# An attention product in fp32 with one set of weights, the mask on VectorE, the shift on GpSimd, a router product with stacked weights, and another opening and order

## The reference, cut to what matters

```python
x = x + tanh(g_xattn) * xattn(LN(x), ctx)
x = x + tanh(g_ffn)  * ffn(LN(x))
# xattn: q = Wq x + bq; k, v = Wk ctx + bk, Wv ctx + bv; 8 heads of 32 channels,
#        each position attends to a window of 16 positions; softmax; Wo out + bo
# ffn, each of the 16*256 rows of 2048 positions is a token:
logits  = flat @ router_weight.T + router_bias      # 64 experts
scores  = softmax(logits); topk_w, topk_idx = top_k(scores, 8)
out     = flat * topk_w.sum() + w_dense @ expert_bias
```

## Time and profile before

| | us |
|---|---|
| median of 3 runs | 1567.97 |
| profiled execution, its time | 1567.15 |
| its span, first to last instruction | 1565.0 |
| PE busy | 1469.5 (94%) |
| PE weight loads busy | 1210.0 (77%) |
| DVE / ACT / POOL busy | 1269.8 / 1148.2 / 1148.8 |
| mean granted TensorE clock | 0.981 |

### The profile page before, as it was taken

One profiled execution on the slowest core, in us unless ns is written; L12 is line 12 of the kernel. 1 busy time (PEld: TensorE's weight loads), 2 busy tenths in 40 slices (PEclk: granted clock), 3 DMA queues, 4 the chain that ended last, 5 costly groups with the idle time before them and its releaser, 6 DMA issues.

```text
span 1565.0 us, 66658 instructions
## 1 busy us (share of the span) xinstructions
PE 1469.5 (94%) x28162; PEld 1210.0 (77%) x28162; DVE 1269.8 (81%) x2970; ACT 1148.2 (73%) x2009; POOL 1148.8 (73%) x1110
## 2 busy tenths in 40 slices
PE   2599999999999999999999999999999999999985
PEld 1477887888888888888888887888888788778764
DVE  4377887889888888988888898888889888888864
ACT  3488777778777877877777787777778787767752
POOL 2487877777787878778787777878777787867762
PEclk8799999999999999999999999999999999999997
DMA  6354455554555455455545545554554555434232
GB/s 202 97 143 125 133 138 133 156 150 102 176 139 136 135 157 142 109 177 139 129 139 157 141 111 179 137 131 137 154 146 110 169 144 132 124 85 132 64 73 93
DMA packets 365577, 210.39 MB, mean 134 GB/s; under 512 B 294497, under 2 KB 295521, under 8 KB 361057
## 3 DMA queue, kind: packets, MB, share of 16 engines
q1 hardware_dynamic: 365280, 206.14, 48.6%
HBM read 136.88 MB, written 33.55 MB: 109 GB/s over the span
## 4 chain that ended last, share of the span: by engine, by line
PE 60%; DVE 26%; issue 7%; POOL 2%; ACT 2%; DMA 1%; SPq 1%; POOLq 0%; DVEq 0%; ACTq 0%
PE ps_j L1099 22%; PE ps_a L1123 9%; PE ps_s L1158 9%; PE ps_s L1099 6%; PE ps_r L1200 6%; DVE prob_t L882 3%; DVE wq_lo L805 2%; PE ps_s L1153 2%; DVE p_sum L872 2%; PE ps_t L1140 2%; PE ps_a L1177 2%; DVE lg L1028 2%; DVE neg_max L861 1%; DVE st_x L889 1%; DVE v_turn L853 1%
## 5 line engine op out<-in xcount | busy, mean ns | idle before, releaser
L474 POOL TENSOR_TENSOR score<-score,p_inv 128x384 f32<-128x384 f32 x256 | 221.8, 867 | 117.2 <-DVE p_inv L876 116.1
L481 POOL TENSOR_TENSOR prob<-score,prob 128x384 f16<-128x384 f32 x256 | 266.1, 1040 | 30.8 <-ACT prob L633 30.0
L1158 PEld LDWEIGHTS ps_s<-kv_win,q_col 32*32 32x32 f32 x16384 | 192.9, 105 | 55.2 <-issue 55.2
L1123 PEld LDWEIGHTS ps_a<-prob_t,v_diag 128*128 128x128 f16 x6528 | 198.9, 97 | 42.3 <-DVE prob_t L882 26.2
L1123 PE MATMUL ps_a<-prob_t,v_diag 128*128 128x64 f16 (+1 forms) x6528 | 212.4, 190 | 19.4 <-DVE prob_t L882 16.0
L1158 PE MATMUL ps_s<-kv_win,q_col 32*32 32x48 f32 x16384 | 228.2, 203 | 1.9 <-issue 1.9
L455 POOL TENSOR_TENSOR c_lo<-c_in,c_hi 128x1024 fp32r<-128x1024 f32 x64 | 152.5, 2382 | 98.6 <-ACT c_hi L607 98.6
L882 DVE STREAM_TRANSPOSE prob_t<-prob 128x512 f32<-128x512 f32 x256 | 176.7, 699 | 54.9 <-POOL prob L481 54.9
L1099 PE MATMUL ps_j<-c_hi,wkv_hi 128*128 128x512 f32 x512 | 170.9, 415 | 39.9 <-POOL c_lo L455 29.9
L450 POOL TENSOR_TENSOR att_lo<-att,att_hi 128x512 fp32r<-128x512 f32 x128 | 162.7, 1275 | 60.2 <-ACT att_hi L593 59.4
L571 ACT ACTIVATE kv_win<-ps_j,v_bias 128x512 f16<-128x512 f32 x128 | 106.5, 844 | 109.7 <-PE ps_j L1099 109.7
(11 more groups left out here) (149 smaller groups left out, 3320.6 us busy)
## 6 DMA issues: line engine op xcount, KB each, us to landing
v_diag<-v_turn SPq DMA_DIRECT2D x512, 68.0 KB, 2.8
c_in<-ctx_dram SPq DMA_DIRECT2D x64, 512.0 KB, 4.8
x_in<-x_dram SPq DMA_DIRECT2D x64, 512.0 KB, 5.6
x_res<-x_dram SPq DMA_DIRECT2D x64, 512.0 KB, 4.4
out_dram<-x SPq DMA_DIRECT2D x32, 1024.0 KB, 7.0
c_sq<-ctx_dram SPq DMA_DIRECT2D x60, 512.0 KB, 5.5
x<-ctx_dram SPq DMA_DIRECT2D x4, 512.0 KB, 6.5
x<-experts_dram SPq DMA_DIRECT2D x2, 512.0 KB, 10.9
```

The lines of the kernel that those rows point to most:

```text
L474: pool.tensor_tensor(score[:, u], score[:, u], p_inv[:, u, :].unsqueeze(2).to_broadcast([P, HALF, KEYS]), ALU.mult).then_inc(pm_rdy, 1)
L481: pool.tensor_tensor(part(prob[:, u % 2], 1)[:, :, 0:KEYS], score[:, u], part(prob[:, u % 2], 0)[:, :, 0:KEYS], ALU.subtract).then_inc(pl_ ...
L1123: ins = pe.matmul(ps_a[g][:, q0:q1], part(v_diag[:, g, j], kv), part(prob_t[:, g, lo:hi], kp), start=(j == 0 and n == 0), stop=(j == NB), ...
L1158: ins = pe.matmul(s[head(h), n * KEYS:(n + 1) * KEYS], q_col[head(h), g, at:at + SUB], kv_win[c % 2][head(h), 0, g, at:at + KEYS], start=F ...
```

## The change

- `attend` uses the whole fp32 words of `v_diag` and `prob_t`: one fp32 matmul for each of the 17 blocks, of 48 columns (all but the first leave out 16 columns that the window never reaches). The f16 halves go, and with them `high`, `low`, `values_low`, the squares of ctx with their loads, `scales` and the rescaled weights of v.
- The mask is no longer a matmul: the bank is opened by a bf16 matmul of zeros of 2 columns, and DVE adds the mask while it copies the scores to SBUF (`masked`); the maximum is taken there, and `shift` goes to POOL.
- The router works on float32r halves: ACT and DVE write `turn_hi` and `turn_lo`, the stationary operand is `wr_both` (high and low weights of the 64 experts side by side), the moving one has 256 columns. The two halves of the result are added by a product with `fold` once a sequence (`logit_sums` on ACT, `fold_logits` on PE).
- The sum of the router's weights is one matmul of a sum made by DVE instead of 16; splitting the experts goes from POOL to ACT and DVE.
- The opening loads v's weights, c_in, k's weights and x first, and waits for no scale. The order on every engine is another, `queries(1)` stands at the end of the step before instead of at the start of its own, and each unit has semaphores of its own.

```diff
 def attend(g, off):
     for j in range(BLKS):
-        lo = max(0, (2 * j - 1) * SUB)
-        q0 = max(0, (j - 1) * SUB)
-        for n, (kv, kp) in enumerate(((0, 0), (1, 0), (0, 1))):
-            ins = pe.matmul(ps_a[g][:, q0:q1], part(v_diag[:, g, j], kv),
-                            part(prob_t[:, g, lo:hi], kp),
-                            start=(j == 0 and n == 0), stop=(j == NB), skip_group_check=True)
+        skip = SUB // 2 if j else 0
+        lo = max(0, (2 * j - 1) * SUB) + skip
+        q0 = max(0, (j - 1) * SUB) + skip
+        ins = pe.matmul(ps_a[g][:, q0:q1], v_diag[:, g, j], prob_t[:, g, lo:hi],
+                        start=(j == 0), stop=(j == NB), skip_group_check=True)
 def scores(u, off):
-    pe.matmul(s[:, 0:HALF * KEYS], ident_b[:], mask[:].rearrange("p n k -> p (n k)"),
+    pe.matmul(s[:, HALF * KEYS:HALF * KEYS + 2], blank[:], blank[:, 0:2],
               start=True, stop=False, skip_group_check=True)
 def router(off):
     for k in range(TB):
-        for g in range(G):
-            ins = pe.matmul(ps_r[:, g * E:(g + 1) * E], x1_t[:, g, k], wr[:, ch * TB + k], ...)
+        for n, v in enumerate((turn_hi, turn_lo)):
+            ins = pe.matmul(ps_r[:, ACC], wr_both[:, ch * TB + k], v[:, k].rearrange("p g c -> p (g c)"), ...)
+def fold_logits():
+    need(pe, acc_rdy, b)
+    for g in range(G):
+        ins = pe.matmul(ps_r[:, LOGITS + g * E:LOGITS + (g + 1) * E], acc[:, g * P:(g + 1) * P], fold[:], ...)
...
 # DVE
-def shift(u):
-    dve.tensor_tensor(score[:, u], scores_of(u), neg_max[:, u, :].unsqueeze(2).to_broadcast([P, HALF, KEYS]), ALU.add)
+def masked(u, off):
+    need(dve, s_mm[u], nth(b, c, off))
+    need(dve, pt_rdy[u], nth(b, c, off - 1))
+    dve.tensor_tensor(score[:, u, :, 0:KEYS], ps_s[u % 2][:, 0:HALF * KEYS].rearrange("p (n k) -> p n k", k=KEYS),
+                      mask[:].unsqueeze(1).to_broadcast([P, HALF, KEYS]), ALU.add).then_inc(mk_rdy[u], 1)
+def turned_low(g, off):
+    dve.tensor_tensor(turn_lo[:, :, g], ps_t[:].rearrange("p (k t) -> p k t", k=TB), turn_hi[:, :, g], ALU.subtract)
...
 # POOL
-def low(u):
-    pool.tensor_tensor(part(prob[:, u % 2], 1)[:, :, 0:KEYS], score[:, u], part(prob[:, u % 2], 0)[:, :, 0:KEYS], ALU.subtract)
+def shift(u, off):
+    pool.tensor_tensor(rows, rows, neg_max[:, u, :].unsqueeze(2).to_broadcast([P, HALF, KEYS]), ALU.add)
...
```

More of the change, by code:

```diff
@@ L33 @@
 BF16 = mybir.dt.bfloat16
-F16 = mybir.dt.float16
 I32 = mybir.dt.int32
@@ L310, in head @@
             return slice(SUB * h, SUB * (h + 1))
[L312 to L316, removed]
         OWN = slice(LEFT, LEFT + CHUNK)
+        wr_staged = x1[1][:, 1, 0:(T // P) * E].rearrange("p (n e) -> p n e", e=E)
+        ex_staged = x1[1][:, 0, :]
+        wo_staged = att[:, :, 0:C]
         block = stack.enter_context(nc.Block())
@@ L513, in step @@
+                if live(b, c, 0):
+                    shift(1, 0)
+                    normalise(0, 0)
+                if live(b, c, -1):
+                    residual(0, -1)
+                    residual(1, -1)
+                if live(b, c, 0):
+                    shift(2, 0)
+                if live(b, c, 1):
+                    x_low(1)
+                if live(b, c, 0):
+                    shift(3, 0)
+                    normalise(1, 0)
                 if live(b, c, 1) or live(b, c, 2):
@@ new lines, in step @@
+                if live(b, c, 0) and live(b, c, 4):
+                    next_stats(0)
+                if live(b, c, -2):
+                    turned_low(1, -2)
+                if live(b, c, 0) and live(b, c, 4):
+                    next_stats(1)
+                if live(b, c, 0):
+                    masked(1, 0)
+                if live(b, c, 0) and c == 3 and seq(b + 1):
+                    ln1(b + 1)
+                if live(b, c, 0):
+                    largest(1, 0)
+                    values_turn(0, 0)
+                    total(0, 0)
+                    invert(0, 0)
@@ L933, in step @@
+                if c == 1 and seq(b - 1):
+                    router_logits(b, 0)
+                if live(b, c, 0):
+                    values_turn(1, 0)
+                if c == 1 and seq(b - 1):
+                    router_logits(b, 1)
                 if finishing(b, c):
                     finish(0)
-                if now:
-                    largest(2)
-                    shift(2)
+                if c == 1 and seq(b - 1):
+                    router_logits(b, 2)
+                if live(b, c, 0):
+                    masked(2, 0)
@@ L1263, in step @@
                     mixture(1)
-                if before:
-                    output(0)
-                    output(1)
-                if now:
-                    scores(3)
+                if c == 1 and seq(b - 1):
+                    fold_logits()
+                if live(b, c, 0):
+                    scores(2, 0)
+                if live(b, c, -1):
+                    output(0, -1)
+                    output(1, -1)
+                if live(b, c, 0):
+                    scores(3, 0)
+                if live(b, c, 2):
+                    values(0, 2)
+                    values(1, 2)
+                if live(b, c, -1):
+                    rows(0, -1)
+                if live(b, c, 2):
+                    keys(0, 2)
                 if finishing(b, c):
@@ L1271, in step @@
                 if live(b, c, 2):
-                    values(0)
-                    values(1)
+                    keys(1, 2)
+                if live(b, c, 1):
+                    queries(0, 1)
                 if finishing(b, c):
@@ L1276, in step @@
                 if live(b, c, 1):
-                    queries(0, 1)
-                if before:
-                    rows(0, -1)
-                if live(b, c, 2):
-                    keys(0)
-                    keys(1)
-                if b == -1 and c == 3:
-                    pe.wait_ge(r_ld, 16 * 4)
-                    for k in range(T // P):
-                        ins = pe.matmul(ps_r[:, 0:E], all_ones[:], wr[:, k], start=(k == 0), stop=(k == T // P - 1))
-                    ins.then_inc(sum_mm, 1)
+                    queries(1, 1)
+                if b == 0 and c == 0:
+                    pe.wait_ge(wrp_rdy, 1)
+                    pe.matmul(ps_r[:, WRSUM], all_ones[:], wr_part[:], start=True, stop=True).then_inc(sum_mm, 1)
             walk(step)
```

1001 lines of the change are left out of this document (441 added, 560 removed).

## The result

| | before | after |
|---|---|---|
| median of 4 runs, us | 1566.43 (1564.26 to 1570.43) | 1841.8 (1838.54 to 1866.02) |
| ratio | | 1.179, 95% interval 1.169 to 1.189 |
| span of the profiled execution, us | 1565.0 | 1838.7 |
| mean granted TensorE clock | 0.981 | 0.919 |

A forecast was written before the change was run, and what follows sets the result against it. The prediction took PE, busy 1469.5 of 1565.0 us, to bound the kernel. Its terms summed to +183 us, span 1748, forecast 1750 us; own range 1700 to 1825, widened to 1855 for the softmax chain.

The forecast's parts named there:

- rival 2: Between scores and attention product, the softmax chain becomes the bound; PE waits 2 us a step, 1878 us; chance 10%.
- rival 3: On PE, load-bound products and transposes make the granted clock fall to its 1.2 GHz level, about 2200 us; chance 8%.
- The prediction's own signs: Right: attend 3.7 to 3.9 us, step near 26, PE above 93% busy. Wrong: steady clock under 0.95, PE under 90%.
- The product (+297): In attend on PE, 34 fp32 records at 112 ns take 3.81 us, 2.32 more than before, 128 times: +297 us.
- The weighed rule: For attend, the skill page's four passes for true FP32 would give 1.36 us; the prediction argued against it from 4-column records.
- Mask (-49): Before the scores on PE, a blank 2-column matmul at 70 ns replaces the 384-column mask matmul, 256 times: -49 us.
- Router (-54): In the router on PE, 8 float32r records taking 0.96 us replace 16 taking 1.81 us, 64 times: -54 us.
- The fold (+19): Once a sequence after the router, 4 records on PE plus a wait for ACT's copy, 16 times 1.2: +19 us.
- New waits (+15): PE waits for att_lo before the output projection, +10, and for ACT in a sequence's last step, +5: +15 us.
- Waits gone (-15): Ahead of attend, PE's 16.0 us of waits for transposed probabilities go, since products come later after their scores: -15 us.
- The opening (-30): At the kernel's start, first projection near 10 us, second chunk's about 26, first scores near 37 instead of 67.21: -30 us.
- Rival 1, the load hides: In attend, the next block's weight load hides under the present matmul, giving 1.87 us and 1502 us in all; chance 5%.

The follow-up runs named there:

- the 64-column kernel: The changed kernel without the skip, fp32 product blocks of 64 columns instead of 48: 1746.3 us, ratio 1.115 to the kernel before.

## Why the prediction was right, and where it was not

**The number.** The direction and the size of the largest term were right for the reasons given. That 1841.8 lies in the range on record is luck in part: the range reached to 1855 for the sake of rival 2, the softmax chain, which did not come, and what came was a part of rival 3, which was placed outside the range at 2200. The prediction's own signs tell it. Of those of being right, the product in steps at full clock, the first scores and the busy share came true; the step of 27.5 us, the router of 1.05 and the blank of 0.10 did not quite. Of those of being wrong one came, a clock under 0.95 in the steady part: it was 0.94. The upper end of all terms together is also added up wrongly, +348 and not +371, which moves nothing else.

- **The product (+297).** Right at full clock, 3.82 us against 3.81. The distances of all products of the 64-column kernel add up to 489 us against 196 before, +293; two of them near the end ran at half clock, and without this it is some +286.
- **The weighed rule.** The Trainium skill's "FP8 and Floating Point Precision", TensorE Precision Notes, has four passes for true FP32. That may be how it is computed, but it does not set the time: 64, 48 and 32 columns take the same 3.8 us, and a single float32r record of 48 columns takes 113 ns, as an fp32 one takes 112.
- **Mask (-49).** The blank matmul costs 829.02 - 828.92 = 0.10 us with the change of shape, not 0.07: -41.
- **Router (-54).** Eight records take 1.05 us instead of 0.96, since the first one costs 0.23: -49 at full clock.
- **The fold (+19).** Right. From 0.12 us behind the start of the last router record to the blank it takes 828.92 - 827.79 = 1.13 us, 16 times: +18.
- **New waits (+15).** Over-sized. `att_lo` comes in time in all but the last step, where PE waits 0.9 us; `x` of ACT costs 4.5 us in 8 waits. At full clock, in the 64-column kernel, `x` costs 7.8 us in 15 waits.
- **Waits gone (-15).** Right: 1.2 us are left of 16.0.
- **The opening (-30).** Right: 38.12 against 67.21, -29, with the steps on the way at 11.76 (forecast near 10), 28.17 (about 26) and 38.12 (about 37).
- **Rival 1, the load hides.** Refuted by all runs: 32, 48 and 64 columns take one time.
- **Rival 2, the softmax chain.** Refuted: DVE is busy for 68%, PE for 96%, and PE waits for `prob_t` once.
- **Rival 3, the clock.** It was the missing part, and the step that failed is the sentence "skipping 16 columns of each block is worth nothing here". In pace it is worth nothing; through the clock it costs 95 us in the changed kernel and 126 in the kernel before. My argument against it was the stretch of the earlier trace rows, 3.5 us at a clock of 1.00. That stretch had 64 columns a record, not 48, and I carried it over as if only the pace counted. The rival was also priced as all or nothing, 2200 us, with every product at half clock; in fact 28 stretches were hit, 229 us.

The Trainium skill's "TensorE: Matmul & The Clock Gate", section HAM oscillation, looks for the cause of a fallen clock in idle gaps of PE. The trace agrees for the stop of 2.40 us of the earlier trace rows, but not for the falls here: PE was busy for all of the 3.70 us looked at ahead of the fall at 847.5, and the measurement decides.

What stays open: why some products are followed by a fall and others not. The two steps shown above have the same instructions at the same pace, and one of them kept its clock. The dependence on the columns is shown for fp32 products, in two orders; float32r was run with 48 columns alone. What makes the clock fall when the columns are few is not shown.

## What to carry to other kernels

Price a record by what its neighbours with the same weights show on both sides, and then ask a second question, which clock it will be granted: a busy PE is not yet a PE at full clock. Where the weight load sets the pace, columns that cost nothing in pace may still be what holds the clock, so cutting them is to be measured, not assumed; here the whole of the loss above the forecast was one line that could be taken back. And a change of many parts is worth splitting: in this one the product cost some 290 us, while the opening alone, taken into the kernel before, made it 0.9% faster.

## What the runs showed that was not expected

- More columns made the kernel faster: 32, 48 and 64 columns a record gave 2080, 1842 and 1746 us with the same number of records and the same 112 ns a record at full clock.
- The clock fell with PE busy throughout, 28 times between 80 and 1780 us of the changed kernel, each time 3.3 to 4.1 us after a product's start, mostly for 3.4 or 13.7 us. At the lower level a product takes 7.1 us.
- One float32r matmul of 512 columns between fp32 blocks takes 0.32 us, in a row of its own kind 0.23, but the blocks behind it take as much less: three of them in a product cost nothing extra (4.49 us against 4.51).
- A single fp32 product of 48 columns a record, with 16 us of other work ahead of it, was enough for the clock to fall.
- With the f16 product PE stopped 27 times, for up to 2.2 us and 27 us in all, with nothing in the records that it waited for.
